# A Mamba-2 stage in head pairs: where in a pair the inter-tile products and the states stand, and in which order VectorE and ScalarE follow

## The reference

```python
proj = hidden_states @ in_proj_w            # gate, x|B|C, dt
hbc = silu(conv4(hbc) + conv_b)             # causal, 4 taps, per channel
cum = jnp.cumsum(dt * A, axis=...)
scores = einsum('cihn,cjhn->cijh', C, B) * exp(cum_i - cum_j) * dt_j   # i >= j
Y_diag = einsum('cijh,cjhp->cihp', scores, x)
states = einsum('clh,clhn,clhp->chpn', decay_states * dt, B, x)
new = chunk_decay * prev + states           # a scan over the chunks
Y_off = einsum('clhn,chpn,clh->clhp', C, prev_states, exp(cum))
hidden = (Y_diag + Y_off + D_param * x) * silu(gate)
out = (hidden * rsqrt(mean(hidden**2) + EPS) * norm_w) @ out_proj_w
```

## Time and profile before

| what | us |
|---|---|
| median of 3 runs | 2167.45 (2167.25 to 2173.0) |
| the profiled execution, its own time | 2167.26 |
| its span in the trace | 2165.5 |
| Mamba pairs, four stretches (273 to 545, 817 to 1087, 1347 to 1620, 1873 to 2148) | 272, 270, 273, 275 |
| attention, feed-forward and starts (the stretches between) | 273, 272, 260, 253 |

### The profile page before, as it was taken

One profiled execution on the slowest core, in us unless ns is written; L12 is line 12 of the kernel. 1 busy time (PEld: TensorE's weight loads), 2 busy tenths in 40 slices (PEclk: granted clock), 3 DMA queues, 4 the chain that ended last, 5 costly groups with the idle time before them and its releaser, 6 DMA issues.

```text
span 2165.5 us, 43621 instructions
## 1 busy us (share of the span) xinstructions
PE 2007.6 (93%) x12940; PEld 1652.1 (76%) x12940; DVE 1610.2 (74%) x2956; ACT 1274.9 (59%) x3110; POOL 785.5 (36%) x1128
## 2 busy tenths in 40 slices
PE   5999989999899998999989999999999999999997
PEld 4888577777688857777778885777778887677776
DVE  4774589999677458888867745888887773588886
ACT  3562388888555227777745513777774552477775
POOL 2210157777300014556530001556661000155565
PEclk9999999999999999999999999999999999999999
DMA  5330233333322002323322200232232220133321
GB/s 188 116 124 1 83 103 131 131 131 126 112 78 75 32 25 74 94 90 87 92 75 87 77 30 17 88 95 87 87 97 83 83 72 1 40 89 94 94 87 54
DMA packets 100366, 180.20 MB, mean 83 GB/s; under 512 B 8337, under 2 KB 30033, under 8 KB 100177
## 3 DMA queue, kind: packets, MB, share of 16 engines
q1 hardware_dynamic: 100304, 179.40, 26.3%
HBM read 139.52 MB, written 39.85 MB: 83 GB/s over the span
## 4 chain that ended last, share of the span: by engine, by line
PE 47%; issue 27%; ACT 11%; DVE 11%; POOL 2%; ACTq 1%; DVEq 1%; DMA 0%; POOLq 0%
PE bank L650 21%; DVE conv_acc L1337 5%; PE bank L893 4%; ACT conv_acc L1101 4%; PE bank L770 4%; ACT place L1183 4%; PE bank L868 3%; PE bank L876 3%; DVE y_in L1467 3%; PE bank L859 3%; PE bank L750 3%; PE bank L778 2%; ACT bank L1190 1%; PE bank L792 1%; DVE place L1472 1%
## 5 line engine op out<-in xcount | busy, mean ns | idle before, releaser
L650 PE MATMUL bank<-xn_r,w_r 128*128 128x512 f32 x2304 | 587.9, 404 | 18.9 <-issue 9.2
L650 PEld LDWEIGHTS bank<-xn_r,w_r 128*128 128x128 f32 x2304 | 421.9, 191 | 113.8 <-issue 24.7
L1337 DVE SCALAR_TENSOR_TENSOR conv_acc<-bank,conv_sb,conv_acc 128x511 f32<-128x511 f32 (+2 forms) x408 | 304.4, 746 | 97.9 <-ACT conv_acc L1101 80.2
L1190 ACT ACTIVATE bank<-bank,cum_neg 128x128 f32<-128x128 f32 x1024 | 288.1, 361 | 47.3 <-PE bank L859 44.2
L1031 ACT ACTIVATE place_r<-bank 128x512 fp32r<-128x512 f32 (+1 forms) x384 | 199.2, 563 | 177.7 <-PE bank L650 151.5
L1269 DVE TENSOR_TENSOR place_r<-bank,place_r 128x512 fp32r<-128x512 f32 (+1 forms) x384 | 231.0, 641 | 87.7 <-ACT place_r L1031 86.7
L650 PE MATMUL bank<-place_r 128*128 128x512 f32 (+3 forms) x1536 | 284.6, 333 | 5.3 <-DVE place_r L1269 4.5
L650 PEld LDWEIGHTS bank<-place_r 128*128 128x128 f32 x1536 | 236.9, 191 | 23.0 <-DVE place_r L1269 9.5
L543 POOL TENSOR_TENSOR carry<-state,dec 128x128 f32<-128x128 f32 x256 | 105.2, 411 | 407.1 <-ACT state L1026 385.6
L517 POOL TENSOR_TENSOR rstd<-var_eps,minus_half 128x4 f32<-128x4 f32 (+2 forms) x12 | 9.7, 807 | 665.9 <-DVE var_eps L1282 665.9
L1055 ACT ACTIVATE place<-bank,bias 128x512 f32<-128x512 f32 (+3 forms) x256 | 131.4, 526 | 161.0 <-DVE bias L1317 161.0
(11 more groups left out here) (142 smaller groups left out, 3544.6 us busy)
## 6 DMA issues: line engine op xcount, KB each, us to landing
w_r<-pair_split SPq DMA_DIRECT2D x96, 512.0 KB, 4.3
w_r<-qkv_split SPq DMA_DIRECT2D x48, 512.0 KB, 4.0
wo_r<-out_split SPq DMA_DIRECT2D x96, 256.0 KB, 2.6
pair_split<-w_r SPq DMA_DIRECT2D x32, 512.0 KB, 3.3
qkv_split<-w_r SPq DMA_DIRECT2D x16, 768.0 KB, 3.8
w_r<-qkv_split SPq DMA_DIRECT2D x48, 256.0 KB, 3.1
raw<-in_w_pair SPq DMA_DIRECT2D x32, 256.0 KB, 3.5
out_split<-wo_r SPq DMA_DIRECT2D x32, 256.0 KB, 2.0
```

The costliest lines, as they stand in the source:

```text
L650: ins = mm(out, lhsT=w(a), rhs=m(b), start=(start and i == 0), stop=(stop and i == 2), **kw)
L1190: ins = A(bank[3 + h][:, c * P:(c + 1) * P], bank[3 + h][:, c * P:(c + 1) * P], ACT.Exp, bias=cum_neg[:, c, bass.ds(n * 2 + h, 1)])
L1337: stt(out=conv_acc[:, back:W], in0=src[:, 0:W - back], scalar=conv_sb[:, ch, TAPS - 1 - back:TAPS - back], in1=conv_acc[:, back:W], op0=AL ...
```

## The change

Nothing is computed in another way, and no instruction is added or removed but for the engines' own bookkeeping. Within a pair, TensorE calls `off_block` right after `turn_x` and `make_states` right after `spread_cum`. ScalarE does `hid_high`, the copy of the states and `squares` before `conv_tanh`, and both `mixes` last. VectorE does `off` before `mixed`, then `total_y` and `gated`, then the three taps in a row, `pair_gate`, and `conv_end` last. GpSimd's and SyncE's lists stay as they are.

```diff
                     turn_x(b, n, par)
+                    if before > 0:
+                        off_block(b, n - 1, 1 - par)
...
                         project_gate(b, n + 1, 1 - par)
-                    if before > 0:
-                        off_block(b, n - 1, 1 - par)
-                    if more:
                         spread_cum(b, n + 1, 1 - par)
+                    make_states(b, n, par)
                     if before > 1:
                         project_out(b, n - 2, par, isinstance(n, int) and n == 2, False)
                     if more:
                         mask_cum(b, n + 1)
-                    make_states(b, n, par)
                     in_block(b, n, par)
...
-                        conv_tanh(K + n + 3)
-                        mixes(n + 1, 1 - par, 0)
+                    if not begin:
+                        hid_high(b, n - 1, 1 - par)
                     act.wait_ge(s_state_done, N + 2)
                     act.wait_ge(s_off_done, N + 1)
                     copy_out(state[:].rearrange("p c q -> p (c q)"), bank[2][:, 0:W - P], s_state_ev)
+                    if not begin:
+                        squares(b, n - 1)
                     if more:
+                        conv_tanh(K + n + 3)
+                        mixes(n + 1, 1 - par, 0)
                         mixes(n + 1, 1 - par, 1)
-                    if not begin:
-                        hid_high(b, n - 1, 1 - par)
-                        squares(b, n - 1)
...
+                    if not begin:
+                        off()
                     dve.wait_ge(s_mix_exp0, N + 1)
                     mixed(par, 0)
                     dve.wait_ge(s_mix_exp1, N + 1)
                     mixed(par, 1).then_inc(s_mix_ready, 1)
-                    if more:
-                        conv_tap(K + n + 3, ch, bank[1], 1)
-                        conv_tap(K + n + 3, ch, bank[1], 2)
-                    if not begin:
-                        off()
-                    if more:
-                        conv_tap(K + n + 3, ch, bank[1], 3)
-                    elif not last:
-                        qk_low(b + 1, 0)
                     if not begin:
                         total_y()
                         gated()
                     if more:
-                        conv_end(K + n + 3, xs[:, 1 - par, :])
+                        conv_taps(K + n + 3, ch, bank[1])
                         if not begin:
                             dve.wait_ge(s_hid_ready, N + 1)
                         pair_gate(b, n + 1, 1 - par)
+                        conv_end(K + n + 3, xs[:, 1 - par, :])
+                    elif not last:
+                        qk_low(b + 1, 0)
```

## The result

| what | before | after |
|---|---|---|
| median, us | 2168.37 | 2221.3 (2221.2 to 2221.41, 4 runs) |
| ratio, 95% interval | | 1.0242 (1.0229 to 1.0255) |
| span of the profiled execution, us | 2165.5 | 2219.6 |
| steady round, sequences 1 to 3, us | 8.75 | 9.20 |

The account below looks back on a forecast made before the run. It took the order of waits around a round through the engines, no engine being full, as the bound. Steady pairs +20, sequence 0 +1, pair 30 +7.5, last pairs +0.8, first pairs -2: +27, 2195 us; range 2168 to 2212.

Parts of the forecast that it names:

- the round of 8.9 to 9.05: Sign to look for: distance in us between successive `turn_x` in sequences 1 to 3.
- the walk: Hand-timed steady pair in the new order, from one `conv_end` to the next: 8.99 us, 0.24 longer than 8.75.
- `total_y` falls due inside `add_squares`: Steady pair: VectorE's `total_y` is held by GpSimd's `add_squares`, ending at 4.43 instead of 3.73, 0.70 us lost.
- 0.89 a step: VectorE's taps in a row, each waiting for the one before, start 0.89 us apart.
- The second rival: Taps follow faster in a row, 0.79 us a step: round 8.79, kernel 2178 us; chance 0.13.
- The meeting of `conv_end` and a carry: Steady pair: `conv_end` meets GpSimd's third carry and ends at 8.95 or 8.99, no later.
- The cover of 0.15: Last carry slips to 0.3 in the next round; `off_block` wants it at 0.47, leaving 0.15 us spare.
- The third rival: Last carry ends later than 0.47 and each round waits, about 9.2 us: +38, kernel 2212 us; chance 0.12.
- Sequence 0: Its 28 steady rounds, `total_y` unheld, `conv_end` ending at 9.1 behind a carry: 0.05 each, +1 us.
- Pair 30: Sequences 0 to 2: `conv_end` to 12.7, 3.1 us more, next pair giving back about 0.6; 3 × 2.5 = +7.5.
- First pairs: No `total_y`, and `turn_x` no longer waits for `pair_gate`: -0.5 us in each of four, -2.
- Last pairs: Last sequence's last two pairs, with `hid_high` ahead of the state copy: +0.8 us.

Follow-up runs that it names:

- e2: Changed kernel with `off` writing its product into PSUM bank 2 and `total_y` reading it there; 2208.37 us, ratio 1.0177.
- e1: Changed kernel with ScalarE's copy of the states moved ahead of `hid_high`; 2210.77 us, ratio 1.0185.
- e3: Changed kernel with `conv_tanh` writing PSUM bank 1 and `conv_end` reading it there; 2202.41 us, ratio 1.0151.
- e13: Changed kernel with GpSimd's small `pick_heads` moved from ahead of `add_squares` to behind it; 2209.2 us, ratio 1.0188.
- e5: Changed kernel with `conv_tanh` ahead of `squares` on ScalarE; 2218.68 us, ratio 1.0226.
- e4: Changed kernel with the edits of e2 and e3 together; 2171.15 us, ratio 1.001.
- e7: Kernel before, in its old order, with e4's two PSUM buffer edits alone; 2157.39 us, ratio 0.9939.
- e6: e4 plus the edits of e1 and e5, so changed order, both PSUM buffers and two ScalarE moves; 2134.04 us, ratio 0.9833.
- e11: Changed kernel with GpSimd's `hid_low` moved behind the next pair's `weigh_x`, ahead of `add_squares`; 2336.16 us, ratio 1.0768.
- e8: Kernel before with TensorE's part of the change alone, ScalarE and VectorE in the old order; 2679.2 us.

## Why the prediction was wrong in size

The direction was right, and the hold on `total_y` that the forecast rests on is there. It does not set the round by itself: freed alone, it gives back 0.18 of the 0.45 (e2). Of the signs named, L1472 at 1.15 in sequences 1 to 3 and 0.55 in sequence 0, TensorE's 0.75 of waiting at `turn_x` and pair 30 at 12 to 13 came; the round of 8.9 to 9.05 did not. The failing step is one sentence: "The last carry then slips to about 9.3, that is 0.3 in the next round, and `off_block` wants it at 0.47: covered by 0.15." The last state ended 0.80 behind the end of `conv_end`, since `conv_end` held the third carry for 0.48, which the walk had put at nothing (0.80 less 0.48 is 0.32, the walk's 0.3); and through `hid_low` and `weigh_x` that delay reached the next `total_y`. Point by point:

- **"`total_y` falls due inside `add_squares`... 0.70 lost".** Right. It was held by 0.60, ending 0.42 behind `add_squares`, as the earlier trace rows gave it. Where the carries don't disturb it (e1, e3) this chain has 9.10 and 9.07, 0.08 to 0.11 above the 8.99 walked.
- **"0.89 a step" for the taps in a row.** Right: 2.52 for three (975.37) is twice 0.89 and one 0.74. The second rival falls in the loop. In the pairs that are written out they take 2.31, 0.78 a step, so its number holds there.
- **The meeting of `conv_end` and a carry.** Mis-sized, and with the sides exchanged. I had `conv_end` wait "8.95 or 8.99, no later". In the run `conv_end` came first by 0.07, and the carry was held, for 0.48. I had added no price for the held GpSimd instruction, though the walk of pair 30 has one: it takes about 0.4 off `xn_low` for what `conv_end` cost it. That reading was right, as the `conv_end` inside `xn_low` before and the undisturbed `xn_low` of the changed kernel show:

```profile
1084.44 1.34 DVE L1346 SCALAR_TENSOR_TENSOR place<-conv_th,conv_acc 128x512 f32<-128x512 f32 x1 [0.80 <-ACT conv_th L1106]
...
1106.15 2.49 POOL L582 TENSOR_TENSOR xn_r<-xn_t,xn_r 128x512 fp32r<-128x512 f32 x2 [4.46 <-ACT xn_r L1068]
```

- **The cover of 0.15.** Wrong, above all since I walked one round from a start without delay. I let the late carry cost something at `off_block` only. In GpSimd's own queue `hid_low` and `weigh_x` stand behind it, without any cover: `weigh_x` started 0.36 behind the multiply instead of 0.18, `add_squares` and the release of `total_y` with it, and so `conv_end` and the next carry. Walked round, loop Q has from `conv_end` to `conv_end` 0.69 + 0.26 + 0.08 + 0.41 + 1.24 + 0.94 + 1.29 + 0.42 + 0.03 + 0.62 + 2.52 + 0.03 + 0.67 = 9.20. These are the trace's own distances, so they must sum to the round; e13 shows that it is this loop.
- **The third rival** gave the round (9.2) and the steady term (+38, measured +37.2) nearly to the letter, but by another path, so the agreement is luck. It has the projections wait for the carries. That loop, P, closes at 9.02 (e2), so by it alone the round would have been set by V's 9.07 to 9.10.
- **Sequence 0**, "+1": measured +3.8. The mechanism was right: `total_y` takes 0.55 there. `squares` waits for `add_squares` (0.29, at 382.5), and `conv_tanh` for it; the round is 9.23, not 9.15.
- **Pair 30**, "to 12.7", a net 2.5 a pair: 12.56 to 12.89. The three pairs cost 9.4, where the walk gave 3 × 3.1 = 9.3. The ends behind them gave back 4.6 instead of 1.8, so the net is +4.9, not +7.5.
- **First pairs**, "-0.5 in each of four": right for pair 0 (-2.1). Pair 1 was not in the sum and cost 5.6: `off_block` waits 0.60 for the last carry of pair 0 (833.11), and `squares` stands ahead of `conv_tanh`; e5, without the latter, has 9.0.
- **Last pairs**, "+0.8": +2.6.

On the lock the Trainium skill (SBUF — State Buffer, "Who interferes with whom") says that a VectorE instruction with two SBUF inputs and a GpSimd instruction that reads SBUF exclude each other for the whole instruction, that the first to issue wins, and that one SBUF input, outside the modes that use both ports, does not contend. The runs agree on the direction, both ways: `conv_end` 0.07 ahead holds the carry, `add_squares` 0.02 ahead holds `gated`. They agree on the remedy too: 0.55 in e2, 0.40 in e3. On the size they differ a little: the held end is 0.42 behind for an instruction of 0.55, and 0.26 behind for one of 0.40.

The forecast was 27 us short: 17.2 of it the steady rounds, 5.6 pair 1, 2.8 sequence 0, 1.8 the last pairs, 2.1 the start of sequence 0, less 2.6 for pair 30.

## What to carry to other kernels

Walk a new order round its loops until the times repeat, through the queues of engines that are mostly idle too: a delay that one engine's slack covers may have no cover on another. When VectorE and GpSimd both read pairs of SBUF operands, list where their windows overlap in the new order, for both of them; writing one operand into a PSUM bank that is free anyway takes the lock away (e4 against the changed kernel: 50 us). Freeing a single one of two tied loops will not show what the pair costs (18 and 13 hundredths of a us apart, 49 together). To judge an order, take the meetings away from both orders: here that left the new one 14 us behind (e4, e7), and only two more moves on ScalarE put it 23 ahead (e6).

## What of the hardware was not expected

- The lock holds GpSimd as well as VectorE, and it turns on 0.07 us. A 0.40 us carry took 0.88 behind a `conv_end` that had started 0.07 earlier, and 0.72 behind one that had started 0.23 earlier (e13). The state behind it, which met nothing, took 0.46.
- `gated` took 1.82 instead of 0.69 behind an `add_squares` that started 0.02 earlier (e11), and 0.89 where it started 0.34 before the end of one (e4): both end 0.55 behind it.
- The loops of e8, in which TensorE waits 2.12 us at one place, lost more than the wait: the granted clock was 0.91 in a stretch of them, and the same twelve matmuls took 4.58 us there instead of 2.98. In pair 30 of the changed kernel TensorE idles 4.44 us. From 1111.90 to 1116.00 the granted clock is then 0.50, the lower of the two levels (1.2 GHz), and the `off_block` of pair 31 takes 1.49 us instead of 0.94.
